# First-layer expert weights in whole 8 KB rows, two units at a time, in a fused graph-transformer and mixture-of-experts kernel on one Trainium2 core

## What is computed

```
logits = x @ Wr + br                      # 8 experts
top_p, top_i = top_k(softmax(logits), 2)
h = relu(x @ W1[e] + b1[e])               # W1: 8 experts x 1024 x 2048
y = h @ W2[e] + b2[e]                     # W2: 8 experts x 2048 x 1024
out = x + sum over the 2 chosen e of top_p * y
```

## Time and profile before

| | |
|---|---|
| median of 3 executions | 1039.89 us (1036.9 to 1041.93) |
| the profiled execution, its own time | 1042.34 us |
| its span, first to last instruction | 1040.6 us |
| PE busy | 996.6 us (96%) |
| DVE busy | 775.1 us (74%) |
| ACT busy | 635.5 us (61%) |
| experts' loads, L458 and L462 | 144 DMAs of 512 KB and 72 of 1024 KB |

### The profile page before, as it was taken

One profiled execution on the slowest core, in us unless ns is written; L12 is line 12 of the kernel. 1 busy time (PEld: TensorE's weight loads), 2 busy tenths in 40 slices (PEclk: granted clock), 3 DMA queues, 4 the chain that ended last, 5 costly groups with the idle time before them and its releaser, 6 DMA issues.

```text
span 1040.6 us, 15023 instructions
## 1 busy us (share of the span) xinstructions
PE 996.6 (96%) x5191; PEld 848.5 (82%) x5227; DVE 775.1 (74%) x1078; ACT 635.5 (61%) x825; POOL 145.0 (14%) x185
## 2 busy tenths in 40 slices
PE   4999999999999999989999899999999999999898
PEld 4898999888889899978788778788787878788675
DVE  7446888867585869767753788888887878788487
ACT  4357777523322133879952667777777787778472
POOL 3003242410001002243320300000000000000013
PEclk9999999999999999989999899999999999999989
DMA  9562342456546763211105499999999999999886
GB/s 313 168 183 83 100 113 70 126 147 173 166 142 182 213 177 117 82 41 42 41 7 201 182 349 381 386 357 371 378 372 374 374 381 359 363 380 385 298 315 232
DMA packets 140508, 237.33 MB, mean 228 GB/s; under 512 B 6908, under 2 KB 48124, under 8 KB 137892
## 3 DMA queue, kind: packets, MB, share of 16 engines
q1 hardware_dynamic: 135780, 225.91, 63.5%
q0 software_dynamic: 1760, 6.37, 1.6%
q10 hardware_dynamic: 2912, 4.34, 1.1%
HBM read 206.56 MB, written 30.03 MB: 227 GB/s over the span
## 4 chain that ended last, share of the span: by engine, by line
PE 78%; DVE 9%; ACT 7%; DMA 3%; issue 2%; SPq 0%; POOL 0%; ACTq 0%; DVEq 0%; POOLq 0%
PE bank L1322 35%; PE bank L971 5%; PE bank L973 5%; PE bank L972 5%; PE bank L985 4%; PE bank L987 4%; PE bank L986 4%; PE bank L1204 2%; DVE wlo L1397 2%; DMA raw<-in_wffn 2%; PE bank L1121 2%; ACT dense L743 2%; PE bank L1048 2%; PE bank L1218 2%; PE bank L1309 1%
## 5 line engine op out<-in xcount | busy, mean ns | idle before, releaser
L1701 DVE TENSOR_TENSOR wlo<-raw,whi 128x2048 fp32r<-128x2048 f32 x72 | 164.6, 2289 | 28.3 <-ACT whi L869 27.9
L869 ACT ACTIVATE a_all<-raw 128x2048 fp32r<-128x2048 f32 x72 | 138.1, 1918 | 52.5 <-DMA raw<-in_wffn 29.0
L869 ACT ACTIVATE whi<-raw 128x2048 fp32r<-128x2048 f32 x72 | 137.9, 1916 | 42.4 <-DMA raw<-in_wffn 23.5
L1397 DVE TENSOR_TENSOR wlo<-raw,whi 128x1024 fp32r<-128x1024 f32 (+1 forms) x72 | 110.4, 1539 | 49.6 <-ACT whi L658 48.4
L658 ACT ACTIVATE whi<-raw 128x1024 fp32r<-128x1024 f32 (+1 forms) x72 | 89.0, 1242 | 90.8 <-PE bank L973 47.7
L1701 DVE TENSOR_TENSOR t_all<-raw,a_all 128x2048 fp32r<-128x2048 f32 x36 | 82.5, 2293 | 40.8 <-ACT a_all L869 40.6
L971 PE MATMUL bank<-a_all,whi 128*128 128x384 f32 x320 | 109.5, 342 | 0.2 <-DVE t_all L1473 0.2
L1322 PE MATMUL bank<-a_all,xg 128*128 128x512 f32 x360 | 106.7, 410 | 1.0 <-DVE t_all L1701 1.0
L973 PE MATMUL bank<-a_all,wlo 128*128 128x384 f32 x320 | 107.2, 335 | 0.0
L972 PE MATMUL bank<-a_all,whi 128*128 128x384 f32 x320 | 107.1, 335 | 0.0
L1322 PE MATMUL bank<-whi,t_all 128*128 128x512 f32 x288 | 100.4, 410 | 0.0
(11 more groups left out here) (276 smaller groups left out, 2041.5 us busy)
## 6 DMA issues: line engine op xcount, KB each, us to landing
raw<-in_wffn SPq DMA_DIRECT2D x144, 512.0 KB
raw<-in_wffn SPq DMA_DIRECT2D x72, 1024.0 KB
raw<-in_wall SPq DMA_DIRECT2D x28, 1024.0 KB
raw<-in_wall SPq DMA_DIRECT2D x32, 512.0 KB
yrows<-zero SPq DMA_DIRECT2D x24, 512.0 KB, 7.0
y_rows<-zero SPq DMA_DIRECT2D x8, 1024.0 KB, 8.7
dense<-yrows SPq DMA_DIRECT2D x8, 512.0 KB, 7.9
y_rows<-dense ACTq DMA_DIRECT2D x16, 256.0 KB, 5.6
```

The source lines that it names most:

```text
L869: act.activation(hi_ring[u % RAW], raw[:, u % RAW, :], ACT.Copy).then_inc(hi_done, 2)
L1397: dve.tensor_tensor(ring(wlo, k), part(k), ring(whi, k).bitcast(F32), ALU.subtract).then_inc(lo_done, width(k))
L1701: dve.tensor_tensor(lo_ring[u % RAW], raw[:, u % RAW, :], hi_ring[u % RAW].bitcast(F32), ALU.subtract)\
```

## The change

Loads of W1 are issued for two units u and u + 1 (u even) at once: two DMAs of 1 MB, each a whole block, 8 KB in one piece per partition, one into slot u % 4 and one into the next. Both slots then hold a half of each unit. SP waits for both slots (2u + 4 in place of 2u + 2), and ACT's wait for an odd unit falls away, since its data lands with that of the even one. Units 8 and 10 wait for one more low part too, as the slot they go to is read by two units. `ring_f` and `raw_f` give the views: 4 runs of 512 numbers, 1024 apart, in place of 2048 in one run.

```diff
+        def ring_f(m, u):
+
+            return m[u % RAW].rearrange("p (j n) -> p j n", j=4)
+
+        def raw_f(u):
+
+            w = u % UNITS
+            if w >= 8:
+                return raw[:, u % RAW, :].rearrange("p (j n) -> p j n", j=4)
+            pair = raw[:, u % RAW - w % 2:u % RAW - w % 2 + 2, :].rearrange("p i (f h n) -> p h (i f) n", f=2, h=2)
+            return pair[:, w % 2]
...
             def unit(g, u, e):
 
-                sp.wait_ge(lo_done, g * F_PIECES + LAYER_PIECES + 2 * u + 2)
                 dst = raw[:, u % RAW, :].rearrange("p (j n) -> p j n", j=4)
-                if u < 8:
-
+                if u < 8 and u % 2 == 0:
+
+                    sp.wait_ge(lo_done, g * F_PIECES + LAYER_PIECES + 2 * u + 4)
                     for i in range(2):
-                        src = wffn[bass.ds(e * UNITS + u // 2 * 2 + i, 1)].rearrange("a p (f h n) -> (a p) f h n", f=2, h=2)
-                        sp.dma_start(dst[:, 2 * i:2 * i + 2, :], src[:, :, u % 2, :]).then_inc(raw_in[u % RAW], 16)
-                else:
+                        src = wffn[bass.ds(e * UNITS + u + i, 1)].rearrange("a p n -> (a p) n")
+                        sp.dma_start(raw[:, u % RAW + i, :], src).then_inc(raw_in[u % RAW], 16)
+                    sp.sem_inc(raw_in[u % RAW + 1], 32)
+                elif u >= 8:
+
+                    sp.wait_ge(lo_done, g * F_PIECES + LAYER_PIECES + 2 * u + (4 if u in (8, 10) else 2))
...
             def hi_f(g, u):
 
-                act.wait_ge(raw_in[u % RAW], g * F_TURNS * 32 + (TURNS * 32 + (u // RAW + 1) * 32))
+                w = u % UNITS
+
+                if w >= 8 or w % 2 == 0:
+                    act.wait_ge(raw_in[u % RAW], g * F_TURNS * 32 + (TURNS * 32 + (u // RAW + 1) * 32))
                 act.wait_ge(used, g * F_PIECES + LAYER_PIECES + SPLIT + 2 * (u - UP))
-                act.activation(hi_ring[u % RAW], raw[:, u % RAW, :], ACT.Copy).then_inc(hi_done, 2)
+                act.activation(ring_f(hi_ring, u), raw_f(u), ACT.Copy).then_inc(hi_done, 2)
...
-                dve.tensor_tensor(lo_ring[u % RAW], raw[:, u % RAW, :], hi_ring[u % RAW].bitcast(F32), ALU.subtract)\
+                dve.tensor_tensor(ring_f(lo_ring, u), raw_f(u), ring_f(hi_ring, u).bitcast(F32), ALU.subtract)\
```

## The result

The changed kernel took 1114.85 us in the median of 4 executions (1112.53 to 1116.8); the kernel before, on the same chip, 1040.91 us (1036.9 to 1044.83). The ratio is 1.0713, 95% interval 1.0688 to 1.0739: 7.1% slower. Forecast were 1101 us and 1076 to 1127.

The account below looks back on a forecast made before the run. PE and DMA were full and the ring had no room; eight passes at 8.1 us give 65, plus 3.6, less 3.4 and 4, so 61 us more: 1101 us, range 1076 to 1127.

Parts of the forecast that it names:

- The turn sets the pass: Expert loop: four turns of a raw slot, 48.56 us without slack, would grow to 56.15 us, 8.1 us per expert.
- turns A and B: Slot 1's turns for units 0 and 1, then 4 and 5: wait, pair transfer and both conversions, 16.35 and 15.30 us.
- turn C: Slot 1's turn for unit 9: unit 8 now leaves together with it, so 13.8 us.
- turn D: Slot 1's turn for unit 13, as before the change: 10.7 us.
- The transfer of a pair: 2 MB of W1 from SP's issue to ACT's start: 8.3 us, bounds 7.3 and 9.0.
- First pass and lead: First expert: pair (6, 7) leaves late, costing 3.6 us; PE's lead over the loads gives 3.4 us back, once.
- The ninth pass: Last pass: 8.1 us more, less 4 us hidden under ACT's 9.75 us idle time before unit 3.
- No gain in rate from the 8 KB pieces: W1 loads: first MB takes 5.0 us in 8 KB pieces against 4.5 us in 2 KB pieces.
- Faster by larger pieces: Rival: larger pieces relieve full DMA engines; best case 1029 us, likelier 1034 to 1039; chance 0.04.
- slower by less: Rival: a pair arrives near 7 us, excess 1 to 5 us per expert, total 1046 to 1077 us; chance 0.11.
- The clock: Rival: PE's clock drops after its stop at turn_h, at most 27 us on top, 1110 to 1130 us; chance 0.12.
- Free edits: Fewer SP issues, added semaphore count and ACT's and DVE's views in four runs: taken as costing nothing.

Follow-up runs that it names:

- e4_copy_first: Changed kernel with ACT's copy of the first bank of h moved ahead of its copy of unit 4: 1112.3 us, ratio 1.068.
- e7_both_8kb: Kernel before, each W1 unit one 1 MB DMA in 8 KB pieces, plain views, plus waits for both slots empty and both full: 1102.03 us.
- e9_empty_8kb: Kernel before, each W1 unit one 1 MB DMA in 8 KB pieces, plus only the wait for both slots empty before issue: 1055.5 us.
- e1_both_2kb: Kernel before with both waits of a pair (empty before issue, full before copy), its loads in 2 KB pieces untouched: 1132.5 us, ratio 1.0883.
- e11_unit8_late: Kernel before with 8 KB W1 units, plain views, both waits of a pair, and units 8 and 10 also waiting for both slots: 1113.43 us.
- e5_rows8k_w1: Kernel before with W1 laid out per unit, each one 1 MB DMA in 8 KB pieces into its own slot, no added wait: 1040.27 us.
- e6_rows8k_all: Kernel before with W1 and W2 laid out per unit, each one 1 MB DMA in 8 KB pieces, no added wait: 1038.14 us.
- e8_both_2kb_one: Kernel before with both waits of a pair, each W1 unit one 1 MB DMA in 2 KB pieces: 1111.27 us, ratio 1.0676.

## Why the prediction was right, and where it was not

**The turn sets the pass: right,** shown by the chain, from which PE is gone, by e4_copy_first, which moved PE's idle time and left the pass, and by the edits to the waits, which lengthened turns A and B, and turn C where unit 8 left late. The equal sums show nothing: also the 48.56 and 48.55 us with which the prediction found that the ring has no room are equal by themselves, as turns laid end to end. What pointed to it was that ACT sat idle before each unit of slot 1 and that SP issued 0.17 us behind each release. The four terms were 16.35, 15.30, 13.8 and 10.7 us, sum 56.15; measured 16.10, 15.06, 13.67 and 11.31, sum 56.15. Two small errors cancelled: the conversions of a pair took 7.71 and 6.59 us where I had summed 7.88 and 6.83, and turn D 0.6 us more than as before. The transfer of a pair, taken as 8.3 us from the one row with such pieces, was 8.40 and 8.47 from the low part, so 8.2 to 8.3 behind the 0.17. In part that is luck too: I had 5.0 us for the first 1 MB and 3.3 for the rest up to ACT's start; in the pair of e7_both_8kb shown above they were 4.25 and about 4.1. The 57 us of seven passes came as 56.8.

The Trainium skill (DMA: Bandwidth & Descriptors, Anatomy of one DMA) gives an estimate of 6.8 us for one DMA of 2.1 MB. The chain has 7.45 us from the second issue alone, so the trace doesn't agree; the fit is for one DMA from GpSimd.

**First pass and lead: mis-sized.** I took 3.6 us for the late pair (6, 7) and gave 3.4 back for PE's lead. By PE's first matmuls, the cut used above, the first pass also holds a turn A, that of the next expert's pair (0, 1), 4 us longer than before; so the forecast has 4.2 us in it, and measured are 6.5. I had priced the lateness at unit 6; PE stopped one unit before, at the second `turn_h`, for the copy that ACT makes behind unit 6. PE's timeline of the changed kernel there, and then ACT's:

```profile
608.02 1.11 PE L1327 MATMUL bank<-ident,dense 128*128 128x128 f32 x4 [4.50 <-ACT dense L918]
```

```profile
605.57 1.91 ACT L887 ACTIVATE a_all<-raw 128x2048 fp32r<-128x2048 f32 x1 [8.23 <-DMA raw<-in_wffn]
607.39 0.58 ACT L918 ACTIVATE dense<-bank 128x512 f32<-128x512 f32 x1
```

This is the stop that I described for pair (4, 5) and did not look for at (6, 7). PE began unit 6 at 612.73, 25.5 us into the pass; before it was 608.45 - 589.09 = 19.4, so 6.1 us late already there. The lead was spent, as assumed: in steady passes PE takes unit 1 0.3 us after its low part, where it took it 3.4 us after the earlier trace rows.

**The ninth pass: wrong.** I had 8.1 us in it less 4 for what ACT's wait for the loaded values would cover, and turn A (about 4 of the 8.1) belongs to the pass before, where pair (0, 1) is loaded. So by the same cut the forecast has next to nothing here, and it cost 8.7. The chain of the changed kernel shows why nothing was covered:

```profile
1042.69 6.16 issue
...
1049.02 1.92 ACT a_all L887
...
1051.03 2.31 DVE t_all L1719
...
1053.50 0.34 SPq L470
...
1054.04 6.69 DMA raw<-in_wffn
```

The unit behind ACT's wait is unit 3, the odd partner. Pair (6, 7) may leave only after its low part, so the transfer starts behind the stall; before, unit 6 left at 979.92, 6 us ahead of the stall's end at 986.05. The new wait made a cover into part of the path. That accounts for some 3 us: PE's unit 6 began 29.3 us into the pass for 26.3 before. The larger part, 5.7 us, came at the last two units. SP issued the last load at 1080.02, and ACT began it at 1095.33, 15.3 us later; before the change it was 9.5 us (1013.84 to 1023.33). The last matmuls then took 4.35 us, at a granted clock of 0.67, where they took about 2.9 at 1.00:

```profile
1099.70 4.35 PE bank L1340 x12
```

GpSimd's gathers ran beside this load. The DMA view of 1080 to 1096, by queue:

```profile
q0 software_dynamic: 864, 3.15, 50.0%
q1 hardware_dynamic: 1106, 2.17, 36.1%
```

But they ran beside it before the change too (46.3% of the engines' time in 1012 to 1024), and the last load took 15.0 us in e9_empty_8kb, with one wait, and 8.6 us in e1_both_2kb, with both. So its length does not follow the change's waits; what sets it was not tried. The ninth pass was 62.8 us in e7_both_8kb, 63.9 in e11_unit8_late and 66.1 in e4_copy_first. How much of these 5.7 us belongs to the change stays open.

Together the first pass is 2.3 us and the ninth 8.6 us above the forecast, and the experts began 1.8 us earlier: these are the 9 us by which the profiled execution was off (70.2 us for 61). The other 5 of the 14 us between 1101 and 1114.85 are how the profiled executions stand to the medians: I took 2.4 us off for the one before, and the one after is 2.3 us below its own.

**"No gain in rate from the 8 KB pieces": wrong for this kernel as changed, right for the one before.** I had compared 5.0 with 4.5 us, two loads in different company. Side by side the larger pieces bring a pair to ACT 0.5 us sooner, which is 9.2 us in all, and one DMA in place of two for each unit is 21.2 us. Without the waits both are worth nothing (e5_rows8k_w1). The forecast was not hurt, since its 8.3 us came from the row with 8 KB pieces; the forecast for e1_both_2kb was.

**Late unit 8 (turn C): right.** I had 13.8 us for it; measured 13.67, and 12.33 without it. It is worth 11.4 us (e11_unit8_late against e7_both_8kb), about a fifth of what the two waits cost (62 us).

**Rivals.** *Faster by larger pieces:* e5_rows8k_w1 and e6_rows8k_all rule it out. The rule of the Trainium skill named there, at least 1 MiB per DMA (DMA: Bandwidth & Descriptors, Rules for kernel authors), shows a gain here only behind the waits: 1132.5 to 1111.3 us with the same waits and pieces; where the queue was full, 1040.9 against 1040.3 us is none. *No change* and *slower by less* are out by the result. *The clock:* PE dropped to the lower level for a few us in every pass, as I had feared. Over the seven passes PE sat idle for 42.0 us of the 56.8 that they grew; the other 14.8, 2.1 a pass, are slower matmuls, so the forecast of 8 us idle in each was about 2 too high. In the loop that cost no time that can be seen: passes at a granted clock of 0.97 took 55.82 and 56.59 us, at 0.94 56.18 and 56.13. At the last unit it cost some 1.5 us. (The working in the prediction has a slip: 0.60 over 8 us comes to 6.4 us at half speed, not 6.8, and to a loss of 3.2 us.) **Free edits: right** (e11_unit8_late).

## What to carry to other kernels

Before widening the unit at which a ring is released, write out one turn of a slot: wait for release, issue, transfer, every conversion that must end before the next release. Then look whether the turn has slack. Measured turns always add up to the pass, so their sum doesn't tell; idle time does. If the converting engine sits idle for the load in each turn, and the issue stands right behind each release, there is none, and what is added to a turn is added to the pass (turn C of e11_unit8_late is 1.25 us longer than that of e7_both_8kb, its pass 1.0 us). "Empty before issue" and "full before use" cost 15 and 24 us alone and 62 together, since only together do they put the whole transfer and all conversions in series. If the pieces of a load are too small, change the layout in memory so that a unit is one piece in its own slot (e5_rows8k_w1, e6_rows8k_all), not the order in which slots are freed; and expect a gain from it only where the queue runs empty: with the queue full the ratios of these two layouts are 1.0006 and 0.9978. Whether a ring with more slots would have hidden the waits was not tried.

## What the runs showed of the hardware

- A 512 KB DMA of 2 KB pieces took SP 0.74 us to the next issue, a contiguous 1 MB DMA in 8 KB pieces 0.53 us, a 1 MB DMA in 2 KB pieces 0.58 us (e8_both_2kb_one). Four DMAs in place of two made a pair 1.4 us (A) and 0.8 us (B) later (e1_both_2kb against e8_both_2kb_one).
- From an empty queue the first 1 MB took 4.25 us in 8 KB pieces and 4.75 us in 2 KB pieces; beyond it both ran near 400 GB/s. With the queue kept full, the size of the pieces changed nothing clear of noise (e5_rows8k_w1, e6_rows8k_all).
- Reading an fp32 tile in four runs of 512 numbers in place of one of 2048, ACT took 1.91 us and DVE 2.29 us, as before.
